# Moving the second norm's sums and root forward, and spreading the feed-forward block's output operations

## The reference

```python
h = layernorm(x) * (1 + ca) + sa
# the mixer
qkv = rms(h) @ w_qkv.T                       # q, k, v: 512 each
w = exp(rms(k))
y = sigmoid(rms(q)) * cumsum(w * v) / (cumsum(w) + 1e-6)
u, g = split(y @ w_swiglu.T)                 # 2048 each
x = x + ga * (h + (u * silu(g)) @ w_out.T)
# the feed-forward
h = layernorm(x) * (1 + cb) + sb             # "the second norm"
gate, up = split(h @ w_gu.T)                 # 1408 each; w_gu is 4 bit values times scales of 128
y = (silu(gate) * up) @ w_down.T
x = x + gb * y / rms_of(y)
```

## Time and profile before

| | us |
|---|---|
| median of 3 runs | 2056.86 (2055.69 to 2057.11) |
| the profiled execution: its time | 2056.17 |
| its span, first to last instruction | 2054.1 |
| PE busy in the span | 1890.7 (92%) |
| DVE, POOL, ACT busy | 1377.6, 952.5, 918.7 |
| one mixer iteration with the second norm (477.13 to 647.72) | 170.59 |
| one feed-forward block, 2 to 5 | 72.03 |

### The profile page before, as it was taken

One profiled execution on the slowest core, in us unless ns is written; L12 is line 12 of the kernel. 1 busy time (PEld: TensorE's weight loads), 2 busy tenths in 40 slices (PEclk: granted clock), 3 DMA queues, 4 the chain that ended last, 5 costly groups with the idle time before them and its releaser, 6 DMA issues. The chain is left out here.

```text
span 2054.1 us, 25337 instructions
## 1 busy us (share of the span) xinstructions
PE 1890.7 (92%) x8376; PEld 829.8 (40%) x8376; DVE 1377.6 (67%) x1773; ACT 918.7 (45%) x1419; POOL 952.5 (46%) x680
## 2 busy tenths in 40 slices
PE   4648999999899999999989999999999999999996
PEld 1213443444344344344434434444344444444332
DVE  6996884874977588487497755733546566566756
ACT  4435324424432432442443351122466766766774
POOL 0554413523432441442342232221587777878974
PEclk8869999999999999999999999999999999999999
DMA  8213111111112011111110101203300111011011
GB/s 306 88 62 115 36 32 54 57 49 57 49 35 77 10 67 34 51 56 48 57 51 33 57 11 47 83 23 121 142 21 1 62 62 44 19 62 42 1 42 62
DMA packets 66881, 119.38 MB, mean 58 GB/s; under 512 B 4720, under 2 KB 28272, under 8 KB 65264
## 3 DMA queue, kind: packets, MB, share of 16 engines
q1 hardware_dynamic: 66800, 118.40, 17.1%
HBM read 80.11 MB, written 38.27 MB: 58 GB/s over the span
## 5 line engine op out<-in xcount | busy, mean ns | idle before, releaser
L585 PE MATMUL bank<-Y,wsw 128*128 128x512 f16 x3072 | 693.9, 383 | 30.0 <-DVE late L943 27.0
L883 POOL TENSOR_TENSOR late<-late 128x512 f16<-128x512 f32 x128 | 194.0, 1516 | 665.5 <-ACT late L736 665.0
L585 PEld LDWEIGHTS bank<-Y,wsw 128*128 128x128 f16 x3072 | 300.8, 98 | 406.0 <-DVE late L943 30.5
L1753 DVE SCALAR_TENSOR_TENSOR f_A<-bank,gu_s,f_A 128x512 f32<-128x512 f32 x352 | 261.9, 747 | 214.9 <-ACT f_A L1571 202.8
L562 PE MATMUL bank<-late,wout 128*128 128x512 f16 x1536 | 352.4, 379 | 8.6 <-POOL late L883 8.5
L1571 ACT ACTIVATE f_A<-bank,gu_s 128x512 f32<-128x512 f32 x352 | 241.7, 688 | 169.2 <-PE bank L1503 155.1
L538 PE MATMUL bank<-H,wqkv 128*128 128x512 f16 x1152 | 262.9, 388 | 38.7 <-DVE H L968 32.6
L1655 POOL TENSOR_TENSOR f_A<-f_A 128x512 f32<-128x512 f32 x176 | 243.7, 1384 | 110.1 <-DVE f_A L1753 109.7
L1467 PE MATMUL bank<-f_HH,f_down_hi 128*128 128x512 f16 x704 | 266.5, 380 | 22.4 <-POOL f_HH L1665 21.7
L943 DVE TENSOR_TENSOR late<-late,bank 128x512 f32<-128x512 f32 x128 | 87.5, 683 | 222.7 <-PE bank L585 216.0
L728 ACT ACTIVATE late<-bank 128x512 f32<-128x512 f32 x128 | 76.4, 597 | 352.8 <-PE bank L585 275.2
(11 more groups left out here) (161 smaller groups left out, 2151.3 us busy)
## 6 DMA issues: line engine op xcount, KB each, us to landing
X<-xT SPq DMA_DIRECT2D x15, 1024.0 KB, 5.6
room<-packed SPq DMA_DIRECT2D x48, 176.0 KB, 2.4
h_scratch<-X SPq DMA_DIRECT2D x8, 1024.0 KB, 4.2
f_X<-x_scratch SPq DMA_DIRECT2D x8, 1024.0 KB, 5.4
x_scratch<-X SPq DMA_DIRECT2D x28, 256.0 KB, 2.1
h_scratch<-SQ SPq DMA_DIRECT2D x28, 256.0 KB, 2.2
outT<-f_X SPq DMA_DIRECT2D x7, 1024.0 KB, 4.2
wout<-wmodT SPq DMA_DIRECT2D x1, 4096.0 KB, 14.3
```

The lines of the kernel that those rows point to most:

```text
L585: mm = nc.tensor.matmul(out[:], wsw[:, pw, k, col:col + P], Y[:, px, k, :], start=(k == 0 and pw == 0 and px == 0), stop=(k == DT - 1 and ...
L883: nc.gpsimd.tensor_tensor(UG[:, j % 2, 1, :], G, UG[:, j % 2, 0, :], ALU.subtract).then_inc(UG_low, 1)
L1753: nc.vector.scalar_tensor_tensor(a, EV[ev_bank(j, m, steps)][:], gu_s[:, which * I_T + j, g:g + 1], a, ALU.mult, ALU.add).then_inc(by_dve, 1)
```

## The change

In the mixer, `n_reduce` moves from after groups 5 and 11 of qkv to after groups 4 and 9. On ACT `n_squares` moves one copy forward and `n_sqrt` from behind the twelve copies to behind the tenth; the splits of tiles 0 and 1 move from step 2 to before step 0, those of tiles 2 and 3 from step 4 to step 1. On DVE `decode_chunk` 1 moves from step 6 to between `n_centre` and `n_scale`, `n_lower` from steps 2 and 4 to steps 0 and 1. On SP the store of chunk 1 and the load of chunk 3 come ahead of the stores of the norm. In the last iteration DVE adds the residual ahead (`wide_h`), so that block 0 of the feed-forward does four operations instead of eight.

In the feed-forward the table of places changes: ACT copies `O` banks 0 and 2, DVE 1 and 3; the adds of the squares go from POOL to DVE; `hidden` of steps 3 and 4 goes from DVE to POOL; the mean moves from place 17 to place 20; inverse, norm and result get places of their own from 23 to 39, where they had 34 to 43 with two operations at places 40 and 41.

```diff
@@ tensor: qkv
-                        if not (isinstance(b, int) and b <= 1) and n in (5, 11):
-                            n_reduce(b - 2, n == 11)
+                        if not (isinstance(b, int) and b <= 1) and n in (4, 9):
+                            n_reduce(b - 2, n == 9)
@@ scalar: s2_copies, iteration
-                    if n == 2 * DT - 2 and not (isinstance(b, int) and b == 1):
+                    if n == DT + 1 and not (isinstance(b, int) and b == 1):
                         n_squares(b - 2)
+                    if n == 2 * DT + 1 and not (isinstance(b, int) and b == 1):
+                        n_sqrt(b - 2)
...
                     sqrt(QSQ, b + 1)
+                    sqrt(KSQ, b + 1)
                     if not (isinstance(b, int) and b == 0):
-                        n_sqrt(b - 1)
-                    sqrt(KSQ, b + 1)
+                        n_split(b - 1, 0)
+                        n_split(b - 1, 1)
...
-                    if s2 and j in (2, 4) and not (isinstance(b, int) and b == 0):
-                        n_split(b - 1, j - 2)
-                        n_split(b - 1, j - 1)
+                    if s2 and j == 1 and not (isinstance(b, int) and b == 0):
+                        n_split(b - 1, 2)
+                        n_split(b - 1, 3)
@@ vector: iteration
                     n_centre(b - 1)
+                    decode_chunk(b, 1)
                     n_scale(b - 1)
...
-                    if s2 and norm and j in (2, 4):
-                        n_lower(b - 1, j - 2)
-                        n_lower(b - 1, j - 1)
...
+                        if j in (0, 1) and norm:
+                            n_lower(b - 1, 2 * j)
+                            n_lower(b - 1, 2 * j + 1)
...
+                        if j >= FT - DT:
+                            wide_h(j - (FT - DT))
@@ feed-forward
-            return range(2, 6) if nxt else range(4, 5) if prev else range(0)
+            return range(2, 6) if nxt else range(5, 6) if prev else range(0)
...
-        COPY_Y, SQUARE_Y, ADD_Y, Y_MEAN = 2 * DT, 9, 10, 17
-        INVERT_Y, NORM_Y, RESULT = 34, 38, 40
-        POOL_STEPS = (1, 2, *range(5, I_T))
+        COPY_ACT, COPY_DVE = {8: 0, 10: 2}, {9: 1, 11: 3}
+        SQUARE_Y = {9: 0, 12: 1, 13: 2, 15: 3}
+        ADD_Y = {13: 0, 15: 1, 17: 2}
+        Y_MEAN, Y_ROOT = 20, 21
+        INVERT_Y = {23: 0, 24: 1, 26: 2, 27: 3}
+        NORM_Y = {29: 0, 31: 1, 33: 2, 35: 3}
+        RESULT = {30: 0, 34: 1, 37: 2, 39: 3}
+        POOL_STEPS = range(1, I_T)
...
+            def copy_y(b, c):
+                dve.wait_ge(down_used, I_T * (b + 1))
+                if not first(b):
+                    dve.wait_ge(out_ready, DT * b)
+                nc.vector.tensor_copy(Y[:, c, :], O[c][:]).then_inc(y_copied[1], 1)
...
-            def mixer_sum(c):
-
-                nc.vector.tensor_tensor(Q[:, c, :], Q[:, c, :], O[c][:], ALU.add).then_inc(last_sum, 1)
-
             def mixer_result(c):
-                dve.wait_ge(last_sum, c + 1)
-                nc.vector.scalar_tensor_tensor(K[:, c, :], Q[:, c, :], mod[:, GA][:, c:c + 1], K[:, c, :],
+
+                nc.vector.scalar_tensor_tensor(K[:, c, :], O[c][:], mod[:, GA][:, c:c + 1], K[:, c, :],
                                                ALU.mult, ALU.add).then_inc(last_ready, 1)
...
-                if first(b) and place < 2 * DT:
-                    (mixer_sum if place < DT else mixer_result)(place % DT)
+                if first(b) and place < 2 * DT and place % 2:
+                    mixer_result(place // 2)
```

More of the change, by code:

```diff
@@ L416, in iteration @@
                 load_words(b, 2)
+                if not start:
+                    store_values(b, 1)
+                    load_words(b, 3)
                 if not start and not last:
@@ L423, in iteration @@
                     load_h(b, 1)
-                store_values(b, 1)
-                load_words(b, 3)
+                if start:
+                    store_values(b, 1)
+                    load_words(b, 3)
                 if last:
@@ L1036, in residual, with wide_h @@
                                                    ALU.mult, ALU.add).then_inc(x1_ready, 1)
+            def wide_h(c):
+                dve.wait_ge(wide_loaded, 32)
+                nc.vector.scalar_tensor_tensor(K[:, c, :], Q[:, c, :], mod[:, GA][:, c:c + 1], K[:, c, :],
+                                               ALU.mult, ALU.add).then_inc(wide_sum, 1)
             def n_centre(b):
@@ L1157, in iteration @@
                             n_lower(b - 1, j - 7)
-                    if j in (0, 6, 10, 11, 12, 14) and not (j == 0 and s2 and norm):
+                    if j in (0, 6, 10, 11, 12, 14) and not (j in (0, 6) and s2 and norm):
                         decode_chunk(b, (0, 6, 10, 11, 12, 14).index(j))
@@ L1360, in ffn @@
         ADD_X, MEAN, CENTRE, SQUARE_N, ADD_N, VARIANCE = 1, 8, 9, 13, 15, 21
[L1361 removed]
         ROOTS = 21
         INVERT_N, SCALE_N, HIGH_N, LOW_N = 22, 26, 28, 30
[L1364 to L1367 removed]
+        COPY_ACT, COPY_DVE = {8: 0, 10: 2}, {9: 1, 11: 3}
[5 more added lines that the diff above has]
+        RESULT = {30: 0, 34: 1, 37: 2, 39: 3}
+        assert RESULT.keys().isdisjoint(NORM_Y.keys())
+        POOL_STEPS = range(1, I_T)
         def now(place, start, step=1):
@@ L1541, in copy_y @@
                     act.wait_ge(out_ready, DT * b)
-                nc.scalar.activation(Y[:, c, :], O[c][:], ACT.Copy).then_inc(y_copied, 1)
+                nc.scalar.activation(Y[:, c, :], O[c][:], ACT.Copy).then_inc(y_copied[0], 1)
             def var_sqrt():
@@ L1583, in beside @@
             def beside(b, s, place, prev, nxt):
-                due, c = now(place, COPY_Y)
-                if prev and due:
-                    copy_y(b - 1, c)
+                if prev and place in COPY_ACT:
+                    copy_y(b - 1, COPY_ACT[place])
                 due, c = now(place, SQUARE_N)
@@ L1589, in beside @@
                     square_n(c)
-                due, c = now(place, SQUARE_Y)
-                if prev and due:
-                    square_y(b - 1, c)
+                if prev and place in SQUARE_Y:
+                    square_y(b - 1, SQUARE_Y[place])
                 due, c = now(place, HIGH_N)
@@ L1597, in beside @@
                     keep_y(b - 1)
-                if prev and place == ROOTS:
+                if prev and place == Y_ROOT:
                     y_sqrt(b - 1)
@@ L1674, in beside @@
                     add_n(c)
-                due, c = now(place, ADD_Y, 2)
-                if prev and due and c < NSUM:
-                    add_y(b - 1, c)
             def iteration(b, s, prev, nxt):
@@ L1724, in low_n, with add_y @@
                                                ALU.add, ALU.subtract).then_inc(H_low, 1)
+            def copy_y(b, c):
[3 more added lines that the diff above has]
+                nc.vector.tensor_copy(Y[:, c, :], O[c][:]).then_inc(y_copied[1], 1)
+            def add_y(b, n):
+                dve.wait_ge(y_squared, DT * b + n + 2)
+                if n:
+                    dve.wait_ge(y_sum, NSUM * b + n)
+                elif not first(b):
+                    dve.wait_ge(y_red, b)
+                nc.vector.tensor_tensor(RSY[:], RSY[:] if n else SQY[:, 0, :], SQY[:, n + 1, :], ALU.add).then_inc(y_sum, 1)
             def norm_y(b, c, y=None):
@@ L1766, in beside @@
                         work(c)
-                for start, work in ((INVERT_Y, invert_y), (NORM_Y, norm_y), (RESULT, result)):
-                    due, c = now(place, start)
-                    if prev and due:
-                        work(b - 1, c)
-                if first(b) and place < 2 * DT:
-                    (mixer_sum if place < DT else mixer_result)(place % DT)
+                for places, work in ((COPY_DVE, copy_y), (ADD_Y, add_y), (INVERT_Y, invert_y), (NORM_Y, norm_y), (RESULT, result)):
+                    if prev and place in places:
+                        work(b - 1, places[place])
+                if first(b) and place < 2 * DT and place % 2:
+                    mixer_result(place // 2)
                 due, c = now(place, LOW_N)
```

21 lines of the change are left out of this document (8 added, 13 removed).

## The result

The changed kernel takes 2027.28 us (median of 4 runs, 2025.45 to 2030.52); the kernel before took 2056.28 beside it (2055.68 to 2057.11, 4 runs). The ratio is 0.986, 95% interval 0.9843 to 0.9878. It is faster, but by 29 us (1.4%) instead of the 56 forecast. The profiled execution of the changed kernel is the slowest of the four: 2030.52, span 2028.7.

The account below looks back on a forecast made before the run. PE was taken as the bound (busy 1890.7 of 2054.1 us). Mixer 38.7 plus feed-forward 17.4 made 56.1 us off 2056.17: 2000.1 for the profiled execution, so a forecast of 2001 us, range 1990 to 2020.

Parts of the forecast that it names:

- the root of k's 0.65: Start of the mixer's `swiglu`: PE's up group starts 0.65 us late for the root of k; this would go.
- half-clock group: Mixer's `swiglu`: group behind the wait for the first `hidden`, at 1.2 GHz, takes 4.03 us instead of 2.59; would go.
- store landing: Rival, mixer: ACT held at step 1 in front of `high`, 9 to 19 us, say 2015; chance 0.14.
- late first `hidden`: Rival, mixer: first `hidden` still 1 to 2 us late and the clock falls behind it, 14 us, 2015; chance 0.08.
- the slower one: Rival, mixer: ACT's wait for the store eats all gain; 2058 at a 12 us landing, beyond it over 2061; chance 0.03.
- the one by which PE's other waits would go too: Rival, mixer: 2 us per iteration of PE waits for POOL in other steps also go, 12 us more, 1989; chance 0.09.
- the feed-forward gives nothing: Rival, feed-forward: DVE's copies and adds put back what the block ends save, 2018; chance 0.07.
- a norm or result of 0.9 to 1.0 ... caught up at the free pairs: Feed-forward places 30 to 39: `take` plus norm or result is 1.6 us against a 1.51 pair, lateness caught up.
- The 2.63 per block at the ends: Feed-forward block ends: 1.20 us lost in step 10 and 1.43 before the next `down` would go, 15.8 over six blocks.
- POOL held by DVE: Rival, feed-forward: norms, results and adds hold POOL's operations, 0.44 us each or their own length, 29 us, 2030; chance 0.04.
- its terms, 7.4 less 2.2 less 2.73: Block 6: DVE work at places 22 to 33 costs 7.4 us; 2.2 lost there and 2.73 at its end saved.
- The middle of the blocks: Feed-forward: middle loses 2.1 us per block before, 1.8 after (copies 0.7, sum 0.55, table loads 0.5); 1.8 saved over six.

Follow-up runs that it names:

- e1: Changed kernel's mixer, without the residual added ahead for block 0, joined to the feed-forward of the kernel before: 2015.81 us, ratio 0.98 to the kernel before.
- e11: e5 with only the root of the second norm put back between the roots of q and k: 2059.09 us, 35.3 more than e5.
- e2: Mixer of the kernel before, with only the residual added ahead, and the changed kernel's whole feed-forward: 2071.14 us, ratio 1.007 to the kernel before.
- e3: Changed kernel with norms at places 28, 30, 32, 34 and results at 36, 38, 40, 42: 2008.07 us, 19.2 less than the changed kernel.
- e8: e5 with norms and results reading one SBUF tile, scale and residual left out, so the output is wrong: 2009.09 us, 14.7 less than e5.
- e4: Changed kernel with block 6 doing inverses, norms and results at late places of its own (34 to 43): 2020.63 us, 6.7 less than the changed kernel.
- e6: e5 with DVE's copies of banks 1 and 3 one place earlier: 2019.64 us, 4.2 less than e5.
- e7: e5 with adds at places 14, 16, 18, mean at 21 (20 in block 6), inverses from 24: 2017.38 us, 6.4 less than e5.
- e5: Changed kernel with DVE's feed-forward loop over blocks 2 to 5 written out, other engines' loops kept: 2023.82 us, 3.5 less than the changed kernel.
- e9: Changed kernel with the edits of e3, e4, e5, e6 and e7 together: 1990.49 us, ratio 0.968 to the kernel before.

## Why the prediction was wrong

**The mixer, step by step, was right.** Forecast 38.7 us, measured 40.8 alone (e1, medians), 6 times 6.75 in the iterations, and 39.4 in the profiled executions (the feed-forward starts at 1412.98 instead of 1452.39). `hidden` was to start 6.96 us after step 0 and started 7.16 after it; the root of k's 0.65 and the half-clock group went; the store did not hold ACT (its median landing is again 2.2); PE's wait on `late` is 3.2 instead of "about 1". Without the root's new place 35.3 of the 40.8 are gone (e11). The two mixer rivals, store landing and late first `hidden`, did not come; nor did the slower one, nor the one by which PE's other waits would go too (an iteration is 163.84, 164.1 was forecast). Nearest came "the feed-forward gives nothing", given 0.07, and it was still too kind: that part alone costs 14.5 (e2).

**The step that failed: "a norm or result of 0.9 to 1.0 ... caught up at the free pairs".** In block 3 they cost 1.6 to 1.8 at places 29, 33 and 37, and 1.1 to 1.3 at 31, 35 and 39, because POOL's `hidden` or `low` is running there; the takes behind them come late, and they are not caught up at the free pairs. The 2.63 per block at the ends did go, as forecast (steps 10 and 0 are 6.04 in e3), but 2.7 came back in steps 8 to 10. Worth: 17.0 us (e3), the largest part of the miss.

The rival "POOL held by DVE" was given 0.04 and had the harm the wrong way round. It read POOL's 1.71 and concluded that the exclusion cost only 0.44, less than an operation's length. But 0.44 is just what was left of a DVE operation that had started shortly before. The price depends on who starts first: a DVE operation of 0.7 costs POOL 0.4 to 0.5 here, a POOL operation of 1.27 costs DVE up to 1.1. That this rival's 2030 lies near the measured time is luck. Its sign, POOL's operations at 1.7 in the last steps, is what e3 shows, the kernel that lost nothing there. And the row that would have told it was there in the kernel before, in the same view of groups:

```profile
L1745 DVE TENSOR_TENSOR f_X<-f_X,f_Y 128x512 f32<-128x512 f32 x32 | 32.1, 1005 | 0.0
```

The mean of 1005 ns hides a median of 684 and a longest of 1751. I took the mean of a mixture for a price. The Trainium skill, "SBUF — State Buffer", section "SBUF: two separate sides", says of the shared ports that whichever starts first "gets the pair for the whole instruction; the other fully blocks". That was weighed against one row and thought too strong; the rows here agree with it in both directions. The 0.54 and 0.28 us by which a held operation of DVE ends after POOL's are what these traces show, for operations of 0.7 and of 0.4. The section names two kinds of DVE operation, those with two SBUF inputs and those in a two-port mode; e8's copies at 0.41 alone fit the second kind, and its reciprocals, which fit neither, were not held.

**Block 6: mis-sized.** Forecast 2.2 slower (bounds 2 faster, 6 slower; its terms, 7.4 less 2.2 less 2.73, make 2.5), measured 6.85 slower. 1.7 of it are held norms (e3), the rest is the pile-up at 22 to 33, gone with e4. The mechanism was right; DVE's operations were costed at 0.95 where held ones stood among them (low halves of 1.7).

**The middle of the blocks: mis-sized.** Forecast 0.3 less, measured 0.85 more (steps 2 to 6 of block 3: 33.99 for 33.14). The copies cost 0.93 per block for 0.7, and that their place could be one earlier was not seen (e6). The sum and the root cost 0.95 more: steps 4 to 6 lose 2.86, 2.0 of it beside the sum, where 1.05 had been allowed; e7 takes 1.55 of a block away. About 6.9 us over six blocks.

**Not in the prediction at all: the branch.** Before, it took 3.0 us at the same place, while DVE still worked off queued results and takes until 1737.19, and its next take could not start until 1739.50 anyway; now DVE has run dry when it comes to it. That is not only a matter of the results that have gone from the last pairs: e3 has one at place 42, DVE stands idle there for 3.60 all the same, and it loses less because its branch is shorter (4.05). So a part of the loss is the uncovered branch and a part its greater length, which is unexplained. Costing the change, I asked what stood beside each operation that moved, but not what the old operations had covered. Worth 3.5 us net in the median (e5), 6.2 in the profiled execution.

**Block 0** was forecast at 2.0; it gave 1.9 beside e1 and 3.6 in the sum above.

In sum, for the profiled executions against the forecast: 17.0 held, 6.2 branch, 3.0 block 6 beyond the held ones, 6.9 middles, less 1.6 in block 0 and 0.7 in the mixer, 30.8; the forecast was 2000.1 and the execution took 2030.5, 30.4 more. What is open is the length of the branch, the 0.35 us by which a written-out block is longer, and the remaining 1.4 us of a block in e9.
